# A gated cross-attention block with a routed FFN: the attention's tiling, transfers and order are rebuilt

## The reference, cut to what matters

```python
q = layernorm(x)
scores = q_h @ k_h.T / 4;  scores = where(causal or mask, -inf, scores)
x = x + tanh(g_xattn) * (softmax(scores) @ v_h @ W.T + b)
z = layernorm(x)
shared = swiglu(z @ w_in.T) @ w_out.T             # hidden 512
routed = sum over the top 2 of 8 experts: p_e * (swiglu(z @ w1.T) @ w2[e].T)
x = x + tanh(g_ffn) * (shared + routed)
```

## Time and profile before

| | us |
|---|---|
| median of 3 runs | 1306.22 (1303.56 to 1309.5) |
| the profiled execution's own time | 1312.65 |
| its span | 1310.9 |
| TensorE busy | 1167.0 |
| VectorE busy | 956.0 |
| ScalarE busy | 493.1 |
| GpSimd busy | 517.8 |

### The profile page before, as it was taken

One profiled execution on the slowest core, in us unless ns is written; L12 is line 12 of the kernel. 1 busy time (PEld: TensorE's weight loads), 2 busy tenths in 40 slices (PEclk: granted clock), 3 DMA queues, 4 the chain that ended last, 5 costly groups with the idle time before them and its releaser, 6 DMA issues.

```text
span 1310.9 us, 22919 instructions
## 1 busy us (share of the span) xinstructions
PE 1167.0 (89%) x7387; PEld 925.0 (71%) x7387; DVE 956.0 (73%) x2413; ACT 493.1 (38%) x908; POOL 517.8 (40%) x501
## 2 busy tenths in 40 slices
PE   1579999999999999889999977279999999999997
PEld 1356776776777777667677755268888888888886
DVE  6467898898897888878988767646666666666665
ACT  3345545545544544444545433132222222222220
POOL 1012225234243342242243325446556556556543
PEclk9889999999999999999999988579999999999999
DMA  6666565565546546446464205332222222222210
GB/s 162 147 148 157 119 155 112 130 153 112 153 116 135 138 119 158 111 114 147 115 144 114 78 17 145 81 75 67 70 68 62 71 70 69 62 69 72 63 34 10
DMA packets 172875, 135.69 MB, mean 104 GB/s; under 512 B 79150, under 2 KB 165457, under 8 KB 172628
## 3 DMA queue, kind: packets, MB, share of 16 engines
q1 hardware_dynamic: 160984, 105.76, 34.1%
q0 software_dynamic: 11776, 28.46, 7.3%
HBM read 84.22 MB, written 51.51 MB: 104 GB/s over the span
## 4 chain that ended last, share of the span: by engine, by line
PE 62%; DVE 16%; issue 9%; DMA 5%; POOL 2%; ACT 2%; SPq 2%; another core or an unknown queue 0%; POOLq 0%; DVEq 0%; ACTq 0%
PE bank L685 15%; PE bank L703 11%; PE bank L622 6%; PE bank L639 6%; PE bank L706 5%; PE bank L545 3%; PE bank L533 3%; PE bank L576 2%; PE bank L507 2%; DMA w2a<-md_dram 2%; DVE gf L1165 2%; PE bank L511 2%; PE bank L598 2%; DVE mx L1106 2%; DVE w2a L1081 1%
## 5 line engine op out<-in xcount | busy, mean ns | idle before, releaser
L703 PE MATMUL bank<-w2a,gh 128*128 x608 | 218.5, 399 | 0.0
L754 ACT ACTIVATE Pt<-bank,pbias 77x512 f32<-77x512 f32 x256 | 160.9, 677 | 135.5 <-PE bank L535 133.0
L706 PE MATMUL bank<-w2a,gl 128*128 x608 | 170.5, 280 | 0.0
L1345 POOL TENSOR_TENSOR x<-x,af 128x512 f32<-128x512 f32 x32 | 42.4, 1326 | 297.8 <-DMA x<-in_x 297.8
L1403 POOL DMA_INDIRECT out<-ot,Pt x76 | 78.8, 1037 | 152.8 <-DVE ot L1240 149.0
L703 PEld LDWEIGHTS bank<-w2a,gh 128*128 128x128 f32 x608 | 114.2, 188 | 25.1
L1106 DVE TENSOR_REDUCE mx<-bank 128x4 f32<-128x308 f32 x256 | 110.3, 471 | 24.5 <-PE bank L511 23.9
L685 PE MATMUL bank<-z2h,w1h 128*128 128x512 f32 x304 | 121.3, 399 | 5.4 <-DVE z2l L886 4.0
L1350 POOL TENSOR_TENSOR gl<-gf,gh 128x512 fp32r<-128x512 f32 x64 | 83.5, 1304 | 102.0 <-ACT gh L792 101.3
L622 PE MATMUL bank<-x2h,winh 128*128 128x512 f32 x256 | 123.6, 483 | 0.0
L685 PE MATMUL bank<-z2l,w1h 128*128 128x512 f32 x304 | 120.5, 396 | 0.0
(11 more groups left out here) (206 smaller groups left out, 2850.5 us busy)
## 6 DMA issues: line engine op xcount, KB each, us to landing
w2a<-xd_dram SPq DMA_DIRECT2D x96, 256.0 KB, 5.8
af<-in_x SPq DMA_DIRECT2D x32, 256.0 KB, 4.2
xd_dram<-w2a SPq DMA_DIRECT2D x32, 256.0 KB, 2.4
xd_dram<-xTl SPq DMA_DIRECT2D x32, 256.0 KB, 2.8
x<-in_x SPq DMA_DIRECT2D x32, 256.0 KB, 5.8
y_dram<-xn SPq DMA_DIRECT2D x32, 256.0 KB, 2.4
y_dram<-res SPq DMA_DIRECT2D x32, 256.0 KB
w2a<-kd_dram SPq DMA_DIRECT2D x96, 77.0 KB, 3.2
```

What stands on the lines that cost most here:

```text
L703: e.matmul(o, gh2[:, c % 2, fc, t * P:(t + 1) * P], w2v[:, bass.ds(val, 1), fc, :, :].rearrange("p o h d -> p (o h) d"), start=fc == 0, st ...
L706: m = e.matmul(o[:, 0, :], gl2[:, c % 2, fc, t * P:(t + 1) * P], w2v[:, bass.ds(val, 1), fc, 0, :].rearrange("p o d -> p (o d)"), start=Fa ...
L754: e.activation(Pt[0:K, 2 * p:2 * p + 2, :], bank_of["sc", b, p][0:K, :].rearrange("k (j t) -> k j t", j=2), ACT.Exp, bias=pbias[:, b:b + 1 ...
```

## The change

- The order: twelve slots an iteration and one iteration more. First moments and norm run one iteration ahead (slots 8 and 11); `att`, `attT` and `proj` of batch i-3 are at slots 2, 6, 10; `norm2`, `x2T`, `logits` move to iteration b+4. One FFN piece stands in each slot. `load_x` moves from the iteration's end to slot 0, behind `kv`. The second load of x, with GpSimd's addition of the bias, moves from `scores` (slot 0) to `att` (slot 2).
- PSUM: ring P has two pairs of banks (maxima, scores, transposed values), S two banks, F two. A maxima step is two matmuls over 64 rows each, in two banks, and two mask matmuls; one reduction of 616 elements, already negated, drains a pair. An exponential takes 1024 elements from two banks, a copy of values 512 from one.
- Queries go from SBUF to SBUF in twelve DMAs a batch, the maxima in four. `Kbd` is filled by eight DMAs for two batches, not by VectorE. `Kst` still goes through DRAM. The padding mask is loaded and converted once (`masks`), GpSimd adds the causal part.
- The first norm runs on ScalarE, with scale and bias that GpSimd prepares (`root` and two more operations); GpSimd also adds epsilon.
- SiLU: ScalarE copies b from PSUM (`bt`), GpSimd multiplies, one FFN part later ScalarE rounds and GpSimd subtracts. `tt` and `bt` have two buffers.

```diff
...
-    for i in range(NB + 3):
-        slots = [[] for _ in range(10)]
+    order += [("load_x", 0, 0), ("load_x", 1, 0), ("load_kv", 0, 0), ("own", 0, 0), ("moments", 0, 0),
+              ("norm", 0, 0), ("masks", 0, 0)]
+    for i in range(NB + 4):
+        slots = [[] for _ in range(12)]
 
         def put(b, stages):
             if 0 <= b < NB:
                 for slot, name, k in stages:
                     slots[slot].append((name, b, k))
 
-        put(i - 3, ((0, "att", 0), (2, "attT", 0), (3, "proj", 0), (5, "norm2", 0), (6, "x2T", 0)))
-        if (i - 3) % 2 == 1:
-            put(i - 3, ((8, "logits", 0), (9, "logitsT", 0)))
-        put(i - 2, ((0, "scores", 0), (1, "scores", 1), (2, "values", 0), (3, "scores", 2), (4, "values", 1),
-                    (5, "scores", 3), (7, "values", 2), (8, "values", 3)))
-        put(i - 1, ((0, "max", 0), (1, "max", 1), (2, "max", 2), (5, "max", 3), (7, "maxT", 0)))
-        put(i, ((0, "moments", 0), (2, "norm", 0), (7, "xT", 0)))
+        put(i - 4, ((1, "norm2", 0), (3, "x2T", 0)))
+        if i % 2 == 1:
+            put(i - 4, ((8, "logits", 0), (11, "logitsT", 0)))
+        put(i - 2, ((1, "scores", 0), (3, "scores", 1), (5, "scores", 2), (5, "values", 0), (7, "scores", 3), (9, "values", 1)))
+        put(i - 1, ((0, "max", 0), (2, "max", 1), (4, "max", 2), (6, "max", 3), (9, "maxT", 0)))
+        put(i - 3, ((2, "att", 0), (6, "attT", 0), (10, "proj", 0)))
+        put(i, ((7, "xT", 0),))
+        put(i + 1, ((8, "moments", 0), (11, "norm", 0)))
         if i % 2 == 0 and i < NB:
-            for slot, name, k in ((0, "kv", 0), (1, "kbd", 0), (4, "kbd", 1), (6, "kbd", 2), (8, "kbd", 3)):
-                slots[slot].append((name, i // 2, k))
-        for slot in range(10):
+            slots[0].append(("kv", i // 2, 0))
+        for slot in range(12):
             for name, b, k in slots[slot]:
                 order.append((name, b, k))
                 if name == "logitsT":
                     logits.add(b // 2)
-            while at["ffn"] < 24 * (10 * (i - 5) + slot) // 20:
+            if slot == 0 and i + 2 < NB:
+                order.append(("load_x", i + 2, 0))
+            while at["ffn"] < 12 * (i - 5) + slot - 5:
...
+            first, count, wide = {"P": (0, 2, 2), "S": (4, 2, 1), "F": (6, 2, 1), "B": (0, 8, 1)}[ring]
+            i = first + wide * (turn[ring] % count)
             turn[ring] += 1
-            bank_of[use] = banks[i]
-            before, user[i] = user[i], use
-            return banks[i], freed(before) if before else (s["dcon"], DCON["idb"])
+            bank_of[use] = ps[:, i:i + 2, :] if wide == 2 else ps[:, i, :]
+            before = user[i]
+            user[i:i + wide] = [use] * wide
+            return bank_of[use], freed(before) if before else (s["dcon"], DCON["idb"])
...
+                e.dma_start(mk_s[n], A["mask_BxS2_if0"][NB // 2 * n:NB // 2 * n + NB // 2, :].partition_broadcast(P)).then_inc(
+                    s["mk"], 16)
...
                 elif stage_ == "kv":
-                    if b >= 2:
-                        e.wait_ge(s["rm"], 2 * G * (b - 1))
-                    e.dma_start(mk[:, h, :, :], A["mask_BxS2_if0"][b * G:b * G + G, :].partition_broadcast(P)).then_inc(
-                        s[f"mk{h}"], 16)
                     e.wait_ge(s["klo"], b + 1)
                     if b >= 2:
                         e.wait_ge(s[f"kd{h}"], 96 * (b // 2))
@@ -401,9 +405,15 @@
                         e.dma_start(kdr[h, n].rearrange("g (c p) k -> p (g c) k", p=P), t[:, :, :].bitcast(F)).then_inc(
                             s[f"kw{h}"], 16)
                     if b == 0:
-                        e.wait_ge(s["dcon"], DCON["ks0"])
+                        e.wait_ge(s["dcon"], DCON["kb0"])
                     if b >= 2:
-                        e.wait_ge(s["sc"], 8 * G * (b - 1))
+                        e.wait_ge(s["mm"], 4 * G * (b - 1))
+                    for n in range(8):
+                        o = slice(16 * n, 16 * n + 16)
+                        e.dma_start(Kbd[o, h, :, :, n % 4, :].rearrange("p g c k -> p (g c) k").bitcast(F),
+                                    khi[o, :, :].bitcast(F)).then_inc(s[f"kb{h}"], 16)
+                    if b >= 2:
+                        e.wait_ge(s["sc"], 4 * G * (b - 1))
                     e.wait_ge(s[f"kw{h}"], 32 * (b // 2 + 1))
                     for r, n in enumerate((0, 1, 0)):
...
-                        e.wait_ge(s[f"xs{h}"], 48 * (b // 2))
-                    for n, t in ((0, xTh), (1, xTl)):
-                        e.dma_start(xd[h, n].rearrange("(c p) t -> p c t", p=P), t[:, h, :, :].bitcast(F)).then_inc(
-                            s[f"xw{h}"], 16)
-                elif stage_ == "max" and k == 0:
-                    e.wait_ge(s[f"xw{h}"], 32 * (b // 2 + 1))
-                    if b >= 2:
-                        e.wait_ge(s["sc"], 8 * (b - 1))
-                    for r, n in enumerate((0, 0, 1)):
-                        e.dma_start(Xs[32 * r:32 * r + 32, h, :, :].bitcast(F),
-                                    xd[h, n].rearrange("(m r) t -> r m t", r=32)).then_inc(s[f"xs{h}"], 16)
+                        e.wait_ge(s["sc"], 4 * (b - 1))
+                    for r, t in enumerate((xTh, xTh, xTl)):
+                        for q in range(4):
+                            dst = Xs[32 * r:32 * r + 32, h, :, :].rearrange("p (c q) t -> p c q t", c=2)[:, :, q, :]
+                            e.dma_start(dst.bitcast(F), t[32 * q:32 * q + 32, h, :, :].bitcast(F)).then_inc(s[f"xs{h}"], 16)
                 elif stage_ == "maxT":
                     e.wait_ge(s["mT"], b + 1)
-                    if b >= 2:
-                        e.wait_ge(s[f"mt{h}"], 16 * (b // 2))
-                    e.dma_start(md[h], mT[:, h, :].bitcast(F)).then_inc(s[f"mw{h}"], 16)
-                    e.wait_ge(s[f"mw{h}"], 16 * (b // 2 + 1))
-                    e.dma_start(Xs[96:KR, h, :, :].bitcast(F), md[h].rearrange("(k m) t -> k m t", k=4)).then_inc(
-                        s[f"mt{h}"], 16)
-                elif stage_ == "scores" and k == 0:
+                    for q in range(4):
+                        e.dma_start(Xs[96 + q:97 + q, h, :, :].bitcast(F), mT[8 * q:8 * q + 8, h, :].bitcast(F)).then_inc(
+                            s[f"mt{h}"], 16)
+                elif stage_ == "att":
...
+                    t, c = k // 2, k % 2
+                    bk, (sem, v) = take("P", "mm", b, k)
+                    e.wait_ge(sem, v)
+                    o = bk[:, :, 0:4 * K].rearrange("p q (h k) -> p q h k", h=4)
+
+                    for q in range(2):
+                        e.matmul(o[:, q], xTh[64 * q:64 * q + 64, h, c, t * P:(t + 1) * P],
+                                 Kbd[64 * q:64 * q + 64, ks, g, c, :, :], start=True, stop=False)
+                    if k == 0:
+                        e.wait_ge(s["first"], b + 1)
+                    for q in range(2):
+                        m = e.matmul(o[:, q], identb[:, :], (pad[:, b, :] if t else first[:, h, :]).unsqueeze(1).broadcast_to([P, 4, K]),
+                                     start=False, stop=True)
+                    m.then_inc(s["mm"], 1)
...
+                elif stage_ == "norm":
+                    e.wait_ge(s["nm"], b + 1)
+                    if b >= 1:
+                        e.wait_ge(s["xT"], b)
+                    for t in range(2):
+                        i = e.activation(xn[:, t, :], xt[:, h, t, :], ACT.Identity, bias=mr[:, 1, t:t + 1],
+                                         scale=rs[:, 0, t:t + 1])
+                    i.then_inc(s["xn"], 1)
...
+                    e.wait_ge(s["sc"], 4 * b + k + 1)
+                    if b >= 1:
+                        e.wait_ge(s["val"], 2 * (b - 1) + k // 2 + 1)
+                    e.activation(Pt[0:K, 4 * k:4 * k + 4, :].rearrange("k (n j) t -> k n (j t)", n=2),
+                                 bank_of["sc", b, k][0:K, :, :], ACT.Exp,
+                                 bias=pbias[:, b:b + 1], scale=0.25).then_inc(s["P"], 1)
                 elif stage_ == "values":
-                    e.wait_ge(s["val"], 4 * b + k + 1)
+                    e.wait_ge(s["val"], 2 * b + k + 1)
                     if b >= 1 and k == 0:
-                        e.wait_ge(s["O"], 2 * b)
-                    e.activation(OT[:, k, :], bank_of["val", b, k][:, 0:S], ACT.Copy).then_inc(s["OT"], 1)
+                        e.wait_ge(s["O"], b)
+                    e.activation(OT[:, 2 * k:2 * k + 2, :], bank_of["val", b, k][:, :].rearrange("p (q t) -> p q t", q=2),
+                                 ACT.Copy).then_inc(s["OT"], 1)
...
-                elif stage_ == "ffn" and k < 16:
+                elif stage_ == "ffn":
                     fc, part = k // 4, k % 4
-                    if part == 1:
-                        e.wait_ge(s["ha"], 4 * b + fc + 1)
-                        e.wait_ge(s["f"], 4 * b + fc)
```

(67 more changed lines are left out.)

240 lines of the change are left out of this document (95 added, 145 removed), and 4 rows, old and new, of the table names.

## The result

The changed kernel takes 1547.26 us (median of 4 runs, 1543.91 to 1551.92) where the kernel before took 1306.82 in the same comparison: ratio 1.184, 95% interval 1.180 to 1.189. Forecast were 1346 us and a range of 1228 to 1380. The direction was right, the size was not.

What follows compares the result with a forecast made beforehand. SyncE's queue, delaying x and GpSimd's work behind it, was to bound the loop: 78 + 597 + 62 = 737 us, +43; beginning 0, behind the loop -5 and -3, profiled about 1353, so 1346 us; range 1228 to 1380.

Steps and rivals of the forecast that it cites:

- 10.4 forecast: Routing's eight scatters on GpSimd, behind the bias addition: 10.4 us more in six pairs of thirteen, 62 us.
- that chain: Even iteration: late x holds GpSimd's bias, low part and product, then ScalarE's rounding and copy; projection at 20, not 16.8 us.
- the sum: Loop after the change: 78 us, thirteen pairs of 45.9 making 597, scatters 62; together 737, +43.
- 0.31 ... and 0.46 are the bounds: SyncE's issue time in us for one small DMA; twelve query issues then end at 19.2 or 21.0 us.
- the forecast's own time line: Twelve slots of the new order at TensorE's prices; an odd iteration ends at 21.6 us, an even one at 19.9.
- X = 14.6: Landing of the residual's x, in us into an even iteration, ends 14 and 18; a pair is X + 31.3, about 45.9.
- The rival that took the upper price (1390): SyncE's queue: issues at 0.46, x landing at 5.8, X = 18, a pair 49.3, +44 more; chance 0.10.
- I take 0: Beginning: mask loads and twelve issues delay first scores, a shorter DRAM round trip helps; -10 to +5 us, taken as 0.
- 20.7 us a batch: TensorE's own work summed from gapless pieces, 41.5 us a pair, leaving some 65 us of stalls over the loop.
- the 19.0 us of TensorE work in the pair's sum: TensorE work from the end of slot 1's FFN piece to the next even iteration, within a pair of X + 31.3.
- the split at 0: Maxima matmuls over 64 partitions, two side by side: -0.5 to +0.6 us a batch, taken as 0.
- the 19 us that I had drawn from it: Key Properties rule that changing the tiling mode drains TensorE: the sum up to 19 us more.

Runs made afterwards that it cites:

- e1: Changed kernel with the residual's x loaded at slot 6 of the iteration before, ahead of the query moves: 1525.07 us.
- e2: Changed kernel with the SiLU product back on VectorE, without ScalarE's copy and GpSimd's product: 1551.91 us.
- e11: Changed kernel with queries and maxima through DRAM, residual's x and keys loaded earlier, and SiLU product on VectorE: 1368.81 us.
- e4: Changed kernel, same DMAs in another order: residual's x at slot 6, next keys at slot 5, maxima moves ahead of the queries': 1377.39 us.
- e7: Changed kernel with queries and maxima through DRAM, residual's x and keys loaded earlier, and maxima matmuls contracting over 128 rows: 1359.36 us.
- e8: Kernel before with only queries and maxima moved SBUF to SBUF, issued where the changed kernel does: 1481.20 us.
- e9: Kernel before, still through DRAM, with query reads cut into twelve and the maxima's read into four: 1310.40 us.
- e12: Kernel before with queries and maxima moved SBUF to SBUF and loads of keys, next x and residual's x at slot 6: 1313.23 us.
- e18: Kernel before with queries and maxima moved SBUF to SBUF, the twelve query moves issued at slot 0 behind all loads: 1290.77 us.
- e16: Kernel before, moves still through DRAM, with only the loads of keys and next x at slot 6: 1303.91 us.

## Why the prediction was right in kind and wrong in size

**Right.** SyncE's queue sets the time; x lands late, and the product, the projection and the FFN stand behind GpSimd; TensorE's gap ahead of the projection is there, 3.0 to 4.3 us in one pair and 10.5 to 12.3 in the next. Six of thirteen pairs have scatters, as forecast, and such a pair is 8 to 9 us longer (10.4 forecast). e1 removed these peaks. The drains (1.108 and 0.796 us for 1.1 and 0.8 taken) and the untouched last stage came out as costed. One link of that chain mattered less than forecast: without GpSimd's products (e2, e11) no time was won.

**Wrong: the price of a small move, and with it a wait that the sum did not have.** The step reads "0.31 ... and 0.46 are the bounds"; measured are 0.64 to 0.70. The sixteen issues at the turn take 9.9 us to the start of the last one (from 448.50 to 458.40), not 4.7 to 6.7. I dated the maxima's last issue but asked only what it does to the keys' load behind it, never when the first scores need the maxima. In the forecast's own time line that is slot 1 of the next iteration, at 21.6 + 1.2 = 22.8 us; with the measured durations the maxima arrive at 15.5 + 9.9 + 1.9 = 27.3, a wait of 4.5, and 4.8 is in the trace. At 0.31 they would have come at 22.1, in time; at 0.46 at 24.1, already 1.3 late, and the sum had no such term. The eight moves of keys took 5.2 us instead of 3.0, and x was issued 4 us later behind the first write of the keys than I had it; it landed 15.3 us behind that write (397.86 to 413.19), where X = 14.6 means 11.1. So the pair was 56 us, not 45.9: 13 pairs by 10 are 130 of the 201 us that the forecast fell short. How these 10 us divide between the maxima's wait, the later x and the lower clock was not measured. The rival that took the upper price (1390) had X at 18 and still not this wait.

**Wrong: the beginning.** "I take 0"; TensorE's weight loads wait 11.6 and 10.1 us ahead of the scores at 56.6 and 81.9 us, each behind such a block, and batch 2 is 32 us later than before. e4 took back 16 of them.

**Wrong: every piece was priced at the full clock.** All terms came from the earlier trace rows, at a granted clock of 0.99. In the changed loop it is 0.86. TensorE is busy 1220.2 us in the whole program, 1167.0 before, and 1179.0 in e4, which has the same instructions as the changed kernel in another order: 41 of the 53 us go with the gaps. From batch 2 to batch 27 an iteration has 23.8 us of busy time and 6.3 idle, before 21.7 and 1.4. The gaps that a sum adds up are not all that they cost.

**Wrong, and small: TensorE's own work.** The pieces were added up to 20.7 us a batch, while the earlier trace rows give 608.41 us busy in 28 iterations, 21.7 each. So at most 38 us of the loop were stalls to be won, not 65, and the 19.0 us of TensorE work in the pair's sum were a little short.

**Wrong: the split at 0.** Measured 0.33 us a batch, 10.7 us (e7), inside the bounds of -0.5 to 0.6. Of the Trainium skill's two rules weighed there (TensorEngine Tiling (Array Packing), Theoretical Speedup and Key Properties), the run's sign agrees with the second: on balance the split lost time, though less than the 19 us that I had drawn from it. What the switch costs and what the packing saves, each for itself, no run shows.

**How the loss divides.** From the changed kernel to e4, order alone: 170 us of the 240 by the times, 156 by the ratios (1.184 and 1.065; e4 ran once). The rest of e4 over the kernel before is 70 to 84: 11 the split; the other parts were not separated. In e4 TensorE waits 1.5 to 3.0 us for GpSimd's low part, 1.1 to 1.5 for the maxima's drain out of a ring of two bank pairs, and scatter iterations are 2 to 3 us longer. That these make up the rest is argued, not shown; no run undid the bank pairs.

**A theory that fell.** After e8 and before e9 I held that small moves are dear as such. e12 and e18 refute it: the same 512 moves, at the same 0.60 us, make the kernel 182 us slower (e8) or leave it where it was (e18, ratio 0.995) by their place in the queue. The changed kernel with its query moves put behind the loads, as in e18, was not run.

## What to carry to other kernels

A block of many small DMAs on one queue is a delay for everything behind it: add up its issue times, list each load behind it, and ask of every one, and of the block's own last move, when its first user needs it. Put such a block where nothing urgent stands behind it, and see first that a load set ahead of it does not itself wait for a late result. Test a suspect part by its place as well as by its presence, and count a gap on TensorE for more than its length where the clock falls behind it.

## What the runs showed of the hardware that was not expected

- A DMA from SBUF to SBUF holds SyncE's queue 0.60 us in the median, 64 KB pieces and 8 KB rows much alike (0.597 and 0.636), at a spacing of 0.64 to 0.70; reads from DRAM into the same places 0.43 for the queries' pieces and 0.25 for the maxima's rows (e9).
- Such a move of 64 KB lands in 2.0 us; the queries' reads from DRAM land in 5.8 in the kernel before (256 KB each), in 2.4 in pieces of 64 KB (e9).
- TensorE's granted clock in the loop was 0.99 in the kernels without long gaps (before, e12, e16, e18), 0.88 in e8 and 0.86 in the changed kernel. There three hidden matmuls took 1.37 us behind a 4.8 us gap; before, at a granted clock of 0.99, they take 0.69.
